# A graph network on one core: the third layer's remainders all on GpSimd, another split of its columns and values, and another order of TensorE's groups

## The reference, cut to what matters

```
Wh = h @ W + b
row, col = (edge_index[0], edge_index[1])
sc = softplus(deg_coeff[0] * deg_v + deg_coeff[1])
Wr = Wh[row];  Wc = Wh[col]
dot = sum(Wr * Wc, axis=-1)
sim = dot / maximum(nr * nc, EPS)              # nr, nc: norms of Wr, Wc
sim_pos = relu(sim);  sim_neg = -relu(-sim)
base = adj_v * sc * (row != col)
prop_pos = segment_sum((base * sim_pos)[:, None] * Wc, row)
prop_neg = segment_sum((base * sim_neg)[:, None] * Wc, row)
coeff = softmax(coeff_param);  scale = softplus(scale_param)
return scale * (coeff[0] * prop_pos + coeff[1] * prop_neg + coeff[2] * Wh)
```

## Time and profile before

| what | value |
|---|---|
| median of 3 runs | 3884.51 us |
| the profiled execution, its own time | 3884.62 us |
| its span on the core | 3882.9 us |
| third layer, first to last group of its matmuls | about 1880 to 2875 us |
| stretch used below, 1985 to 2865 us | 880 us, 297 groups, 2.963 us each |
| busy over the span: PE, DVE, ACT, POOL | 3024.9, 3187.8, 2164.4, 1348.8 us |
| mean granted TensorE clock | 0.924 of full speed |

### The profile page before, as it was taken

One profiled execution on the slowest core, in us unless ns is written; L12 is line 12 of the kernel. 1 busy time (PEld: TensorE's weight loads), 2 busy tenths in 40 slices (PEclk: granted clock), 3 DMA queues, 4 the chain that ended last, 5 costly groups with the idle time before them and its releaser, 6 DMA issues.

```text
span 3882.9 us, 125317 instructions
## 1 busy us (share of the span) xinstructions
PE 3024.9 (78%) x50473; PEld 2698.4 (69%) x50473; DVE 3187.8 (82%) x6939; ACT 2164.4 (56%) x5734; POOL 1348.8 (35%) x1644
## 2 busy tenths in 40 slices
PE   0288888888888869899777777777765888778876
PEld 0167777777777669899677777677755777777775
DVE  7599999999999823233799999999976889888886
ACT  5323333333333410001688788788765888888887
POOL 2000000000000000000487787787772555555554
PEclk9999999999999989999899999999986888888887
DMA  8156666666666779889677677677746888888884
GB/s 212 55 166 209 207 206 209 207 207 209 209 208 208 241 293 369 338 330 328 214 244 235 222 243 232 225 247 232 229 140 219 272 259 263 265 269 261 262 259 146
DMA packets 655937, 907.64 MB, mean 234 GB/s; under 512 B 363977, under 2 KB 587882, under 8 KB 636411
## 3 DMA queue, kind: packets, MB, share of 16 engines
q1 hardware_dynamic: 633240, 800.64, 64.1%
q10 hardware_dynamic: 19763, 94.38, 6.4%
q0 software_dynamic: 2352, 4.52, 0.6%
HBM read 651.96 MB, written 247.40 MB: 232 GB/s over the span
## 4 chain that ended last, share of the span: by engine, by line
DVE 38%; PE 32%; DMA 11%; ACT 9%; issue 8%; SPq 2%; POOL 1%; ACTq 0%; DVEq 0%; POOLq 0%
PE ps L626 8%; PE ps L964 7%; DVE U L754 5%; DMA U<-AD 3%; DMA A<-ROWS 3%; DVE EDG L777 3%; DMA T<-ROWS 3%; DVE U L1271 3%; DVE EDG L1300 3%; DVE U L1263 2%; PE ps L1178 2%; PE ps L1190 2%; PE ps L1171 2%; DVE U L1634 2%; SPq L1398 2%
## 5 line engine op out<-in xcount | busy, mean ns | idle before, releaser
L542 ACT ACTIVATE U<-ps 128x512 bf16<-128x512 f32 (+1 forms) x637 | 359.1, 573 | 666.1 <-PE ps L638 665.9
L1148 POOL TENSOR_TENSOR EDG<-U,edge 128x256 f32<-128x256 f32 x343 | 244.0, 711 | 850.8 <-DVE edge L1296 732.4
L1466 ACT ACTIVATE U<-U,T 128x65 f32<-128x65 f32 x1806 | 459.9, 340 | 86.0 <-PE ps L1554 81.4
L1178 PE MATMUL ps<-U 128*128 128x65 bf16 x7203 | 300.1, 198 | 217.7 <-DVE edge L1274 215.0
L487 POOL DMA_INDIRECT U<-REC,nod x49 | 48.8, 996 | 1160.7 <-PE ps L582 1038.5
L964 PE MATMUL ps<-U 128*128 128x192 bf16 x4802 | 416.5, 247 | 38.4 <-DVE U L1041 19.3
L964 PEld LDWEIGHTS ps<-U 128*128 128x128 bf16 x4802 | 401.6, 98 | 46.8 <-DMA U<-AD 24.2
L1178 PEld LDWEIGHTS ps<-U 128*128 128x128 bf16 x7203 | 261.2, 101 | 241.3 <-DVE edge L1274 237.4
L777 DVE TENSOR_TENSOR EDG<-edge,EDG 128x896 bf16<-128x896 bf16 x686 | 408.3, 621 | 10.0 <-DMA OSD<-EDG 9.0
L1492 POOL TENSOR_TENSOR U<-U 128x455 f32<-128x455 f32 x258 | 276.2, 1071 | 305.6 <-DVE U L1634 305.6
L651 PE MATMUL ps<-EDG,U 128*128 128x193 bf16 x2401 | 312.8, 252 | 62.0 <-ACT U L542 40.4
(11 more groups left out here) (302 smaller groups left out, 7328.1 us busy)
## 6 DMA issues: line engine op xcount, KB each, us to landing
U<-AD SPq DMA_DIRECT2D x98, 1568.0 KB, 8.7
U<-ROWS SPq DMA_DIRECT2D x343, 448.0 KB, 4.4
OND<-EDG SPq DMA_DIRECT2D x343, 224.0 KB
OSD<-EDG SPq DMA_DIRECT2D x343, 224.0 KB
AD<-U ACTq DMA_DIRECT2D x49, 1568.0 KB, 6.4
EDG<-ROWS SPq DMA_DIRECT2D x343, 224.0 KB, 5.1
U<-OND SPq DMA_DIRECT2D x303, 224.0 KB, 5.3
EDG<-OSD SPq DMA_DIRECT2D x189, 224.0 KB, 4.6
```

The costliest lines, as they stand in the source:

```text
L542: ev4.by(act.activation(prow[i % NPW][:, P * g:P * (g + m)], ps[4 + gg % 2][:, 0:P * m], ACT.Copy))
L1178: ins = pe.matmul(ps[2 + h][:, 65 * k:65 * k + 65], rw[r][:, 2 * P * k:2 * P * k + P], Ws[:, j, s_, 0:65], start=(s_ == 0), stop=(s_ == 2))
L1466: ins = act.activation(V4[k % NV][:, 0, c, :], H[d % 3][:, s, :], ACT.Copy, scale=a4[d % 2][:, s:s + 1])
```

## The change

- Remainders: DVE's instruction is gone. POOL does the remainder of all 7 cells in one instruction and waits for ACT's values and its own.
- Values: KA goes from 3 to 5, so ACT does 5 cells of a group and POOL 2.
- Columns: ACT does every 5th group instead of every 3rd, DVE the other four.
- PE: iteration n is now targets(n+1), spread(n-11), sources(n+1).
- Coefficient: with b the cosine, p*max(b,0) + q*min(b,0) is written as (p-q)*max(b,0) + q*b; two instructions over 49 cells take the place of three, and the head gets one 128x1 subtraction.

```
--- before.py
+++ after.py
@@ -133,6 +133,10 @@
             assert start + n <= 20800
             return U[:, start:start + n]
 
+        def on(s, o):
+
+            return Sem(s.at, o)
+
 
         dv, ac = sem("dve_step"), sem("act_step")
 
@@ -359,6 +363,8 @@
             dv.by(dve.tensor_tensor(sc[:, 15:16], sc[:, 14:15], sc[:, 12:13], ALU.mult))
             dve.wait_ge(dv.at, dv.n)
             dv.by(dve.tensor_scalar(sc[:, 16:19], sc[:, 8:11], sc[:, 15:16], None, ALU.mult))
+            dve.wait_ge(dv.at, dv.n)
+            dv.by(dve.tensor_tensor(sc[:, 19:20], sc[:, 16:17], sc[:, 17:18], ALU.subtract))
             dv.by(dve.tensor_tensor(Wst[D:P, :], Wst[D:P, :], wtmp[D:P, :], ALU.add))
             dv.by(dve.tensor_tensor(W2c[:, D:P], W2c[:, D:P], small[:, 0:D], ALU.add))
             dv.by(dve.tensor_tensor(brow[:, 0, :], brow[:, 0, :], small2[:, 0:D], ALU.add))
@@ -1085,25 +1091,21 @@
         NOS = len(osp)
         OSn = [o.bitcast(BF16).rearrange("p (c r) -> p c r", r=P) for o in osp]
         Wc = part(upper, 2 * NB * 65).rearrange("p (a b f) -> p a b f", a=2, f=65)
-        KA = 3
+        KA = 5
         rows_ld = [sem(f"rows_ld{i}") for i in range(NR)]
         hot_a, hot_d = sem("ends_hot_act"), sem("ends_hot_dve")
         c_got, r_got, c_ev, r_used = sem("c_got"), sem("r_got"), sem("c_ev"), sem("r_used")
         coef, vm_a, vm_p, spr, coll = sem("coef"), sem("value_act"), sem("value_pool"), sem("spread"), sem("collected")
         os_ld = [sem(f"os_ld{i}") for i in range(4)]
 
-        def on(s, o):
-
-            return Sem(s.at, o)
-
-        rem3, low3, rem3p = on(hid, NB), on(relu, NB), on(outp, NB)
+        rem3, low3 = on(outp, NB), on(relu, NB)
         p3_t, p3_ev, p3_mm, p3_out = sem("p3_t"), sem("p3_ev"), sem("p3_mm"), sem("p3_out")
         att, t5_st, ax_st = sem("att"), sem("t5_st"), sem("ax_st")
         NLAST = 49 * (NGB - 1) + 63 + 10 + 4 * (GB - 1) + 1
 
         def by_act(n):
 
-            return n // 3 + 1
+            return n // 5 + 1
 
         def due3(n):
 
@@ -1150,17 +1152,17 @@
                 m = n - 9
                 if 0 <= m < NG:
                     pool.wait_ge(vm_p.at, m + 1)
-                    rem3p.by(pool.tensor_tensor(V3[m % 4][:, 1, KA:G, :], V3[m % 4][:, 0, KA:G, :], S3[m % 4][:, 0, KA:G, :], ALU.subtract))
+                    pool.wait_ge(vm_a.at, m + 1)
+                    rem3.by(pool.tensor_tensor(V3[m % 4][:, 1, :, :], V3[m % 4][:, 0, :, :], S3[m % 4][:, 0, :, :], ALU.subtract))
                 m = n - 10
                 if 0 <= m < NG:
-                    pool.wait_ge(rem3p.at, rem3p.o + m + 1)
                     pool.wait_ge(rem3.at, rem3.o + m + 1)
                     low3.by(pool.tensor_tensor(V3[m % 4][:, 2, :, :], V3[m % 4][:, 1, :, :], S3[m % 4][:, 1, :, :], ALU.subtract))
 
         def pairs3_pe(pe):
-            def ends(n):
-                r, h, j, i0 = n % NR, n % 2, n // NQ, G * (n % NQ)
-                if n % 3:
+            def targets(n):
+                r, h, i0 = n % NR, n % 2, G * (n % NQ)
+                if n % 5:
                     pe.wait_ge(hot_d.at, n + 1 - by_act(n))
                 else:
                     pe.wait_ge(hot_a.at, by_act(n))
@@ -1171,6 +1173,9 @@
                         ins = pe.matmul(ps[h][:, 65 * k:65 * k + 65], rw[r][:, 2 * P * k + P:2 * P * k + 2 * P], Ws[:, i0 + k, s_, 0:65],
                                         start=(s_ == 0), stop=(s_ == 2))
                 c_got.by(ins)
+
+            def sources(n):
+                r, h, j = n % NR, n % 2, n // NQ
                 if n >= 2:
                     pe.wait_ge(r_used.at, n - 1)
                 for k in range(G):
@@ -1191,12 +1196,15 @@
                 spr.by(ins)
 
             pe.wait_ge(ws_o.at, NGB)
-            ends(0)
+            targets(0)
+            sources(0)
             for n in range(NLAST):
                 if n + 1 < NG:
-                    ends(n + 1)
+                    targets(n + 1)
                 if 0 <= n - 11 < NG:
                     spread(n - 11)
+                if n + 1 < NG:
+                    sources(n + 1)
                 b, g, _ = due3(n)
                 if b is not None:
                     project_pe(pe, b, W3s, (6, 7), 2 * NGB + b // GB + 1, p3_t, p3_ev, p3_mm, p3_out)
@@ -1205,7 +1213,7 @@
 
         def pairs3_act(act):
             def columns(n):
-                if n % 3 == 0:
+                if n % 5 == 0:
                     r = n % NR
                     act.wait_ge(rows_ld[r].at, 16 * (n // NR + 1))
                     ac.by(act.activation(rw[r], rw[r], ACT.Abs, bias=negp[:, 0:1]))
@@ -1285,25 +1293,18 @@
                 dve.wait_ge(dvf.at, dvf.n)
                 dvf.by(dve.tensor_tensor(b_, b_, c_, ALU.mult))
                 dve.wait_ge(dvf.at, dvf.n)
-                dvf.by(dve.tensor_scalar(a, b_, 0.0, sc[:, 16:17], ALU.max, ALU.mult))
-                dvf.by(dve.tensor_scalar(c_, b_, 0.0, sc[:, 17:18], ALU.min, ALU.mult))
+                dvf.by(dve.tensor_scalar(a, b_, 0.0, sc[:, 19:20], ALU.max, ALU.mult))
                 dve.wait_ge(dvf.at, dvf.n)
-                dvf.by(dve.tensor_tensor(a, a, c_, ALU.add))
+                dvf.by(dve.scalar_tensor_tensor(a, b_, sc[:, 17:18], a, ALU.mult, ALU.add))
                 dve.wait_ge(dvf.at, dvf.n)
                 if j >= 2:
                     dve.wait_ge(vm_a.at, NQ * (j - 1))
                     dve.wait_ge(vm_p.at, NQ * (j - 1))
                 coef.by(dve.tensor_tensor(d_, a, E3v[:, :, j, 2], ALU.mult))
 
-            def remainder(m):
-                dve.wait_ge(vm_a.at, m + 1)
-                rem3.by(dve.tensor_tensor(V3[m % 4][:, 1, 0:KA, :], V3[m % 4][:, 0, 0:KA, :], S3[m % 4][:, 0, 0:KA, :], ALU.subtract))
-
             for n in range(4):
                 columns(n)
             for n in range(NLAST):
-                if 0 <= n - 9 < NG:
-                    remainder(n - 9)
                 if n < NG:
                     products(n)
                     if n % NQ == NQ - 1:
```

21 lines of the change are left out of this document (10 added, 11 removed).

## The result

| | before | after |
|---|---|---|
| median | 3882.59 us (20 runs, 3871.60 to 3888.62) | 3873.14 us (20 runs, 3861.03 to 3888.09) |
| ratio | 1 | 0.9981, 95% interval 0.9972 to 0.9990 |
| span of the profiled execution | 3882.9 us | 3878.7 us |
| groups of the third layer in 1985 to 2865 us | 297, 2.963 us each | 301, 2.92 us each |

A forecast was written before the change was run, and what follows sets the result against it. DVE was taken to bound the third layer; with work moved, three engines meet at about 748 us, plus 27 for coupling is 775, 105 less. 3884.6 - 105 - 5 = 3774.6, put at 3777 us, range 3742 to 3838.

The forecast's parts named there:

- What bounds the kernel before: Third layer: DVE, busy 843.8 of 880 us, sets the time; work taken off it comes off the end.
- the signs that would prove the forecast wrong: Third layer's 297 groups over 810 us or under 745, PE waits over 40 for POOL's low part, columns' mean past 1.1.
- the sum: Third layer: DVE 2.51, ACT 2.51, POOL 2.52 us a group meet at about 748 us; with 27 added, 775.
- the coupling term: Third layer: three equal engines can't all run without gaps; 3.5%, 27 us, with bounds 0 and 12% (90 us).
- The layer's start: The 42 groups before the profiled stretch took 104 us, 2.48 each; 5 us to be saved.
- the second rival: POOL's remainder waits for ACT's values after a column pair; 1.5 us lost every 5 groups, some 3840 us; chance 0.19.
- Two arguments against it: DVE's remainder had the same wait, 14.2 us in all; ACT makes columns four groups ahead, hiding a 5 us burst.
- the port: DVE and POOL share one SBUF port pair, locked per instruction; 0.3 us a column instead of 0.2, adding 24 us.
- The term for the columns: DVE's columns beside POOL: 238 x 0.1 = 24 us more, with bounds 0 and 105 us.
- ACT and POOL: Third layer: ACT busy 714 us, POOL 691; POOL's wait for coefficients, 58 us, remains, giving POOL 749 us.
- PE's order: PE: the spread, moved ahead of the wait for DVE, fills part of its gaps; counted as nothing.
- The third rival: PE stands 2.7 us per burst and 1.4 per row ahead of the sources, holding DVE; 3917 us, 32 slower; chance 0.04.

The follow-up runs named there:

- The small low part: The changed kernel with POOL's low part over 1 cell of 7, the other six cells' third part left out: 3833.97 us, 0.9881.
- the passes apart: The changed kernel with ACT's two passes over the columns one iteration apart: 3814.42 us, 0.9822.
- the low part first: The changed kernel with POOL's low part ahead of its remainder in an iteration: 3828.91 us, 0.9865.
- the kernel without the burst: The changed kernel with ACT's two column passes cut to 8 of 1792 values: 3802.31 us, 0.9794.
- the run with the slow form: The changed kernel with DVE's column instruction reading and writing its values in steps of 896: one run, 4721.9 us.
- the version with both repairs: The changed kernel with ACT's passes one iteration apart, POOL's low part ahead of its remainder, KA = 4 and ACT's columns every fourth group: 3788.90 us, 0.9766.
- The two reorderings together: The changed kernel with ACT's column passes one iteration apart and POOL's low part ahead of its remainder: 3807.98 us, 0.9815.
- the kernel of 3821 us: The changed kernel with the split of before (KA = 3, ACT's columns every third group), remainders on POOL and PE's new order: 3821.45 us, 0.9846.

## Why the prediction was wrong

**What bounds the kernel before** was right: DVE, and its waits and busy times were read as they are. The moved remainders with the shorter coefficient gave 49 us. Of the signs that would prove the forecast wrong two came: 297 groups take 868 us (over 810), and PE waits 117 us for the low part (over 40). The third did not: the columns' mean is 1.064, over the 0.9 to 1.0 that was expected but under 1.1.

**The step that failed is the sum, in two of its terms.** In the stretch 297 groups took 868 us instead of 775, 93 more. DVE's own busy time is 803 of these instead of 747 (or 748, where the three engines met), some 55 more, and it is idle for 65 us instead of the 27 of the coupling term, 38 more. The layer's start, put at 5 us of gain, lost two groups, some 6 us, with the granted clock at 0.87 where it was 0.95.

**The first term is the coupling**, the 27 us for three engines that meet at 748 us. I named the second rival's mechanism, and it is the one that decided more than half of the miss, but I gave it 0.19 and 1.5 us in five groups; in the turn shown it is 2.76 us, and in 880 us 132 us for 60 column pairs, 2.2 each. Two arguments against it were wrong. That the same wait had cost DVE's remainder only 14 us said nothing: DVE was the slowest engine and ran behind ACT's values, so their lateness was hidden; POOL runs close behind. (Where POOL is itself the slowest, with three values on ACT, its wait is 27 us and less.) And four groups of lead for the columns do not help the values, which stand ahead of them in ACT's queue in one iteration and behind them in the next. I compared sums of work per engine (all near 2.5 us) and did not follow one group around the ring: ACT's values, POOL's remainder, the older low part behind it, the spread, now the sources behind that, targets, ACT's copy. The small low part shows that such a ring, and not any engine's sum, can give 2.82 us, and the passes apart and the low part first show what it cost here: 64 of the 102 us between the forecast and the measurement went with the two of them.

**The second term that was mis-sized is the port**, DVE's price of running beside POOL. Columns were put at 0.98 us; they took 1.064, and 1.129 in the kernel without the burst. What I left out entirely is the small work: four of DVE's five other coefficient instructions became longer too, all but the reciprocal. The new one took 0.505 us (0.25 assumed), the last 0.548 where its like took 0.246 before, and the addition L1319 0.618 where L1318, its like, took 0.352 before. All coefficient instructions of a row sum to 3.09 us, where the seven before made 2.38. The term for the columns, counted as there above their 0.878 of before, was 24 us with a bound of 105; it measured (1.064 - 0.878) x 241 = 45 us, and (1.129 - 0.878) x 237 = 59 in the 815 us of the kernel without the burst. A DVE column and a POOL value that were held up, in a stretch of the changed kernel (their shortest take 0.67 and 0.39 us; the first two records start within 0.02 us, so which came first they don't tell):

```profile
1945.39 1.44 DVE L1271 TENSOR_SCALAR U<-U,iotap 128x1792 bf16<-128x1792 bf16 x1
```

```profile
1945.41 0.93 POOL L1160 TENSOR_TENSOR EDG<-EDG 128x448 f32<-128x448 f32 x1
1946.30 0.78 POOL L1150 TENSOR_TENSOR EDG<-U,edge 128x128 f32<-128x128 f32 x1
```

The Trainium skill's rule that the prediction weighed there (SBUF — State Buffer, "Who interferes with whom": the second to issue blocks fully) is borne out by the trace, 1.44 us beside 0.68, and by the run with the slow form, where GpSimd's 0.39 us became 3.67. The assumption that went with it, a hold-up that grows with POOL's share, is not: the mean was 0.881 with POOL at 97%.

**ACT and POOL.** ACT's busy time was 722 us for 301 groups (714 forecast for 297), POOL's value 0.505 (0.50) and first remainder 0.965 (0.96): these were priced well. The low part took 1.059 instead of 0.96, so POOL's work came to 722 us for 297 groups instead of 691; its wait for coefficients, 58 us in the sum, was only 14.

**PE's order** was counted at nothing. It is worth 7 us in the kernel before and 16 in the version with both repairs, and costs 17 in the changed kernel, where it puts the sources behind a late POOL. The third rival's place was right, its size was not: the wait it names was 117 us, and DVE's own waits for the sources' rows were 23.

In short: 0.9717 of the kernel before by the sum, 0.9981 measured, 102 us apart. The two reorderings together, with all work kept, take away 64 us of that, and the run without the burst 73; so much is shown to hang on the burst and the ring. In both of these DVE is then busy 97% of the time and more, at some 2.66 us a group instead of the 2.51 of the sum. The remaining 29 to 38 us fit DVE's longer instructions, and so the hold-ups at the port; the one run meant to take these away did not, so that part is argued, not shown. The two shares can't be separated cleanly either, since the columns became longer in both runs.

## What to carry to other kernels

When work leaves the one full engine and several meet at the same sum, the sums no longer tell the time: follow one item around the ring of waits, with the longest uneven piece in it, and see what stands behind each waiting instruction in its queue. An old wait's cost says little about the same wait on another engine, if the old engine was the slow one. Where such a ring shows, the cheap repairs are orders within a queue: put what others wait for ahead of what itself waits (45 us here), and cut a long piece so that the short urgent ones pass between (62 us). They need not add up (64 us together): behind the ring stands the next engine's own time, and the longer instructions of two engines that hold each other up belong in its sum.

## What the runs showed of the hardware

A VectorE instruction over 128 x 1792 bf16 values that takes 0.68 us undisturbed took up to 1.44 us beside GpSimd's instructions, GpSimd's 0.39 us became 0.78 us beside it, and VectorE's last coefficient instruction, over 128 x 49 values, took 0.24 us at its shortest and 0.90 at its longest. The column's mean was 1.064 us with GpSimd busy 83% of the time and 0.881 with 97%. The same 1792 values in steps of 896 took 4.2 to 5.0 us, six to seven times the plain form, and in the two cases shown GpSimd was shut out until it ended. TensorE's granted clock was 0.99 where its idle time came as 240 short waits (127 us in all before the spread, the longest 2.2 us, in the kernel of 3821 us) and 0.94 in the kernel before, where 115 waits held 185 us, the longest 5.6.
